# Moving the preparation of the v weights from GpSimd to VectorE in an adaLN attention and FFN block

## The reference

```
mod = (silu(c) @ wmod).reshape(B, 6, 1, 256)           # sa, ca, ga, sb, cb, gb, one set per batch
ga, gb = sign(g) * max(|g|, 0.25)
h = layernorm(x) * (1 + ca) + sa
q, k, v = split(h @ w_qkv + b_qkv)                     # 8 heads of 64
attn = softmax(q^T k / sqrt(64))                       # 64 x 64 per head, summed over the 2048 tokens
out = (v @ attn) @ w_fc + b_fc + h
x = x + ga * (layernorm(out) * gamma + beta)
h = layernorm(x) * (1 + cb) + sb
xr, xk = mu * h + (1 - mu) * h_previous_token
x = x + gb * sigmoid(xr @ W_r) * (relu(xk @ W_k)^2 @ W_v)
```

## Time and profile before

| what | value |
|---|---|
| median of 3 runs | 690.74 us (690.01 to 690.99) |
| profiled execution | 690.6 us, of which the span of the trace is 688.9 us |
| PE busy | 670.7 us, 97% of the span |
| DVE busy | 561.0 us, 81% |
| ACT busy | 393.8 us, 57% |
| POOL busy | 317.5 us, 46% |

### The profile page before, as it was taken

How to read it: one execution, slowest core, us unless ns; L and a number is a source line. 1 busy time by engine, 2 the same in 40 slices (tenths; PEclk the granted TensorE clock), 3 DMA queues, 4 the chain that set the end, 5 groups by cost and what they waited for, 6 DMA issues and landing times.

```text
span 688.9 us, 11754 instructions
## 1 busy us (share of the span) xinstructions
PE 670.7 (97%) x3712; PEld 539.4 (78%) x3712; DVE 561.0 (81%) x1254; ACT 393.8 (57%) x871; POOL 317.5 (46%) x520
## 2 busy tenths in 40 slices
PE   7988999999999999999999999999999999999896
PEld 6777886888778887879868887788878788687674
DVE  5693999789887998889887898979988898658973
ACT  1424575566754675474855667546754747547662
POOL 5272864573254642565335742646325753214320
PEclk9989999999999999999999999999999999999999
DMA  8849345485836666572855849366665528628225
GB/s 316 232 152 222 103 131 123 77 212 97 209 74 142 163 135 147 99 167 92 198 113 79 219 91 213 67 141 158 145 136 99 107 72 173 123 37 179 37 31 91
DMA packets 90984, 93.02 MB, mean 135 GB/s; under 512 B 4224, under 2 KB 89000, under 8 KB 90960
## 3 DMA queue, kind: packets, MB, share of 16 engines
q0 software_dynamic: 33264, 33.03, 32.6%
q1 hardware_dynamic: 55344, 55.97, 25.6%
q10 hardware_dynamic: 2352, 3.73, 1.5%
HBM read 42.84 MB, written 33.10 MB: 110 GB/s over the span
## 4 chain that ended last, share of the span: by engine, by line
PE 86%; DVE 7%; POOL 2%; DMA 2%; issue 1%; ACT 1%; SPq 0%; DVEq 0%; POOLq 0%
PE work L1335 14%; PE work L1318 14%; PE att L1285 13%; PE gram L1267 11%; PE gram L1398 4%; PE att L1370 4%; PE work L1151 4%; PE tr L1260 4%; PE work L1153 4%; PE work L1152 4%; PE tr L1302 4%; PE att L1389 2%; PE gram L1380 1%; PE att L1318 1%; DVE st L907 1%
## 5 line engine op out<-in xcount | busy, mean ns | idle before, releaser
L471 POOL TENSOR_TENSOR rs<-ve,neg_half 128x4 f32<-128x4 f32 x32 | 41.6, 1300 | 161.4 <-DVE ve L917 161.4
L1285 PE MATMUL att<-m_sb,z_t 128*128 128x256 f32 x496 | 112.4, 380 | 1.6 <-issue 0.8
L1335 PE MATMUL work<-mx,w_k_t 128*128 128x512 f32 x236 | 106.2, 592 | 0.0
L1285 PEld LDWEIGHTS att<-m_sb,z_t 128*128 128x128 f32 x496 | 92.4, 190 | 16.9 <-issue 5.7
L1318 PE MATMUL work<-w_r_t,mx 128*128 128x256 f32 x464 | 105.7, 381 | 0.0
L1318 PEld LDWEIGHTS work<-w_r_t,mx 128*128 128x128 f32 x464 | 85.9, 190 | 11.1
L1267 PE MATMUL gram<-z 128*128 128x256 f32 (+1 forms) x512 | 90.7, 331 | 0.0
L1267 PEld LDWEIGHTS gram<-z 128*128 128x128 f32 x512 | 81.1, 194 | 6.9
L934 DVE SCALAR_TENSOR_TENSOR mx<-t_buf,mu_col,h2t 128x512 f32<-128x512 f32 x120 | 84.3, 765 | 1.1
L654 ACT ACTIVATE sq<-att 128x256 f32<-128x256 f32 x124 | 46.1, 383 | 64.1 <-PE att L1285 64.1
L1335 PEld LDWEIGHTS work<-mx,w_k_t 128*128 128x128 f32 x236 | 44.8, 190 | 44.1 <-issue 42.6
(11 more groups left out here) (170 smaller groups left out, 1283.6 us busy)
## 6 DMA issues: line engine op xcount, KB each, us to landing
x_in<-in_L_attn_x_dram SPq DMA_DIRECT2D x32, 512.0 KB, 4.8
x<-rows SPq DMA_DIRECT2D x32, 512.0 KB, 3.4
x<-in_L_attn_x_dram POOLq DMA_DIRECT2D x32, 512.0 KB, 8.9
out_dram<-x SPq DMA_DIRECT2D x31, 512.0 KB, 5.1
out_dram<-y POOLq DMA_DIRECT2D x29, 512.0 KB, 6.2
rows<-row_scratch SPq DMA_DIRECT2D x16, 128.0 KB, 4.1
rows<-row_scratch SPq DMA_DIRECT2D x8, 256.0 KB, 3.8
wqkv_sb<-in_L_attn_w_qkv_dram ACTq DMA_DIRECT2D x1, 1536.0 KB, 9.7
```

Of the source, the lines that this page charges most:

```text
L1285: ins = mm(att_banks(j, alone)[q][:, (t % 2) * D:(t % 2 + 1) * D], z_t[:, j, k, t * P:(t + 1) * P], m_sb[:, k], start=(k == 0), stop=(k == ...
L1335: ins = mm(k_banks(alone)[dh][:], w_k_t[:, ch, rows_dh], mixed(j, alone)[1][:, ch], start=(ch == 0), stop=(ch == KD - 1))
```

## The change

`prep_wv` for batches 1 to 7 goes from GpSimd's list to VectorE's. There it stands behind `low_k(b, 1)` and ahead of `stats_2(b, 3)`, in all of rows 0 to 6. Batch 0 keeps its preparation on GpSimd (`prep_wv()`, `bias_wv()`). In rows 0 to 5 VectorE's steps for batch n + 1 are put in another order among those around the softmax.

```
             def row_steps(b, first, far):              # GpSimd
...
-                    prep_wv(n)
...
-                if first:
-                    prep_wv(n)
...
+            def prep_wv(b):                            # VectorE
+                dve.wait_ge(ca_loaded, 16 * (b + 1))
+                wait_past(dve, m_ready, b)
+                nc.vector.tensor_tensor(wv_aug[:], wv_t[:], rows[:, 3].unsqueeze(1).to_broadcast([P, NP, D]),
+                                        ALU.mult).then_inc(wv_step, 1)
+                dve.wait_ge(wv_step, 2 * b + 1)
+                nc.vector.tensor_tensor(wv_aug[:, :, 0:LAST], wv_aug[:, :, 0:LAST],
+                                        wv_aug[:, :, LAST:D].to_broadcast([P, NP, LAST]), ALU.subtract).then_inc(wv_step, 1)
+                dve.wait_ge(wv_step, 2 * b + 2)
+                nc.vector.tensor_copy(wv_aug[:, :, LAST], vb_col[:, :, b]).then_inc(wv_ready, 1)
...
                 low_k(b, 1)
+                prep_wv(n)
                 stats_2(b, 3)
-                if far:
-                    stats_a(n + 1, 0)
                 gate_o(b, 1)
                 softmax_dif(n)
                 if far:
-                    stats_a(n + 1, 1)
+                    stats_a(n + 1, 0)
                 softmax_norm(n)
                 if far:
+                    stats_a(n + 1, 1)
                     make_z(n + 1, 0)
+                    stats_a(n + 1, 2)
                     make_z(n + 1, 1)
-                    stats_a(n + 1, 2)
                 low_k(b, 2)
                 make_m(n)
```

More of the change, by code:

```diff
@@ L485, in fill_x2, with prep_wv, bias_wv @@
                 nc.gpsimd.dma_start(x2[:, j], x_v[b, j], accum_op=ALU.add).then_inc(x2_filled[j], 16)
[L487 to L495, removed]
+            def prep_wv():
+                pool.wait_ge(w_copied, 2)
+                pool.wait_ge(row8_b_ready, 1)
+                pool.wait_ge(ca_loaded, 16)
                 nc.gpsimd.tensor_tensor(wv_aug[:], wv_t[:], rows[:, 3].unsqueeze(1).to_broadcast([P, NP, D]),
                                         ALU.mult).then_inc(wv_step, 1)
-                pool.wait_ge(wv_step, 2 * b + 1)
+                pool.wait_ge(wv_step, 1)
                 nc.gpsimd.tensor_tensor(wv_aug[:, :, 0:LAST], wv_aug[:, :, 0:LAST],
                                         wv_aug[:, :, LAST:D].to_broadcast([P, NP, LAST]), ALU.subtract).then_inc(wv_step, 1)
-            def bias_wv(b):
-                pool.wait_ge(wv_step, 2 * b + 2)
+            def bias_wv():
+                pool.wait_ge(wv_step, 2)
                 pool.wait_ge(vb_ready, 1)
-                nc.gpsimd.tensor_copy(wv_aug[:, :, LAST], vb_col[:, :, b]).then_inc(wv_ready, 1)
+                nc.gpsimd.tensor_copy(wv_aug[:, :, LAST], vb_col[:, :, 0]).then_inc(wv_ready, 1)
             def add_y(b, j, alone=False):
@@ L571, in _ @@
                 rstd_a(0, j)
-            pool.wait_ge(w_copied, 2)
-            pool.wait_ge(row8_b_ready, 1)
-            centre_wv(0)
+            prep_wv()
             rstd_a(1, 0)
             rstd_a(1, 1)
-            bias_wv(0)
+            bias_wv()
             for j in range(CH):
```

## The result

The kernel after takes 698.62 us (697.52 to 700.22, 4 runs) against 690.75 us (690.01 to 690.99, 4 runs). The ratio is 1.0114, 95% interval 1.0101 to 1.0127: slower by 7.9 us. The direction was forecast. The size was not: 695.7 with a range up to 698.0.

What follows compares the result with a forecast made beforehand. TensorE's list was taken to bound the kernel. In rows 0 to 5 a late `k_lo` costs TensorE 1.12 us less a vanished wait of 0.29: 6 x 0.83 = +5.0 us, forecast 695.7, range 690.2 to 698.0.

Steps and rivals of the forecast that it cites:

- TensorE bounds, and only its waits count: In a row TensorE is busy 80.16 of 80.20 us; VectorE or GpSimd work counts only where TensorE waits.
- The gain on `make_z` at the row's start is worth nothing: VectorE's `make_z` no longer meets GpSimd's v weights and gets back some 2.5 us; effect on time taken as 0.
- The v weights take 2.6 us on VectorE: Behind `low_k(b, 1)`, two instructions of 1.22 us and a small copy, 2.6 us; bounds 1.4 and 5.3.
- `softmax_dif` 1.08 late, the statistics of chunk 0 behind it: On VectorE, `softmax_dif` ends at 358.85, then chunk 0's statistics; the softmax keeps 0.7 us of slack.
- Two `rstd_a` in a row: On GpSimd behind chunk 0's statistics: first 2.31 us to its power, second 1.85; the second value is there at 366.48.
- The second `make_z` beside the DMA issues, 2.13: On VectorE ahead of `low_k(b, 2)`, 2.13 us beside GpSimd's two DMA issues; bounds 1.30 and 3.9.
- The rival at 706: VectorE is blocked for the whole of GpSimd's DMA issues, `k_lo` 2.9 us late, 706 us; chance 0.02.
- What comes back: `m_sb` starts only 0.59 us later, so TensorE's 0.29 wait at `ffn_out(b, 3)` disappears; net 0.83 a row.
- The sum: Rows 0 to 5 at 0.83 us each, +5.0 us; row 6, row 7 and the setup 0.
- The range: 8 in 10: 690.2 to 698.0; the forecast case's own 693.5 to 697.8, with the chain right to 0.35 us a row.
- not slower: Rival: second `make_z` misses the DMA issues and takes 1.30, so `low_k(b, 2)` is on time; 690.7 us, chance 0.21.

Runs made afterwards that it cites:

- e2: Kernel before with only the new order of VectorE's statistics and normalisations, v weights still on GpSimd: 692.77 us, ratio 1.0027.
- e5: Kernel after with the statistics of chunk 2 put ahead of the first `make_z`: 696.84 us, ratio 1.0083.
- e3: Kernel after with GpSimd's `add_y(b, 1)` and `fill_x2(n, 1)` moved behind `rstd_a(n + 1, 2)`: 694.02 us, ratio 1.0052.
- e8: Kernel before with `low_k(b - 1, 3)` put ahead of `prep_qk(n)`, v weights still on GpSimd: 690.22 us, ratio 0.9986.
- e7: e6 with `low_k(b - 1, 3)` put ahead of `prep_qk(n)` at the row's start: 689.29 us, ratio 0.9971 to the kernel before.
- e6: Kernel after with `make_z(n + 1, 1)` moved from in front of `low_k(b, 2)` to the row's end: 691.05 us, ratio 0.9996.
- e1: Kernel after with the old order of statistics and normalisations, v weights still on VectorE behind `low_k(b, 1)`: 695.51 us, ratio 1.0071.
- e4: e1 with the v weights on VectorE moved to the row's start, behind `make_z(n, 2)`: 694.06 us, ratio 1.0045 to the kernel before.

## Why the prediction was right in direction and wrong in size

- **TensorE bounds, and only its waits count**: right. Its busy time is unchanged, and its waits in front of `ffn_out(b, 2)` in rows 0 to 5 (1.24, then 1.39 to 1.41) sum to 8.2 us, against 7.5 more of span.
- **The gain on `make_z` at the row's start is worth nothing**: right. It came (65.1 to 49.9 us in all) and moved no wait: ahead of the next `make_x2` VectorE is idle (2.44 us at 397.55, for `rs_o`).
- **The v weights take 2.6 us on VectorE**: right, 357.35 - 354.68 = 2.67, two at 1.22.
- **`softmax_dif` 1.08 late, the statistics of chunk 0 behind it**: right, 358.90 in place of the 358.85 forecast. The softmax kept its slack, no wait at `wv_attn`.
- **Two `rstd_a` in a row**: the first took 366.17 - 363.87 = 2.30 to its power (2.31 forecast). **The second is the step that failed**: it was priced by one that ran "alone", at 1.85, and took 2.22. In the new order its first operations run beside the first `make_z` (2.22 in e2 as well). e5 puts statistics beside them and gets 1.89. That is 0.37 of the 0.53 by which `k_lo` was later than I said (370.45 against 369.92).
- **The second `make_z` beside the DMA issues, 2.13**: the mechanism was right (e3: 1.40 without them), the size was 2.24 to the next instruction, 0.11 more. With 0.05 from the v weights that makes the 0.53. The rival at 706, by which VectorE stands until the second issue ends, was not borne out: `make_z` ended at 372.62, and the second issue at 371.19 + 1.82 = 373.01. The Trainium skill (SBUF — State Buffer, Who interferes with whom) has the loser of the shared ports fully blocked for the whole instruction of the other; beside these issues the trace does not agree, and `make_z` took 2.21 where it takes 1.38.
- **What comes back**: TensorE's wait is 1.64 in place of 1.12. `m_sb` is 1.10 later (373.86 - 3.49 = 370.37) in place of 0.59. The wait in front of `ffn_out(b, 3)` is gone, as forecast, but for 0.21 in row 1. In row 4 the pair of `k_lo` starts at 392.54 and ends at 393.82, and the load at 393.94 has no idle time before it (lines below the list). Yet only 0.21 of the 0.29 came back. From `attention(4, 1)` at 390.87 to the Gram products at 398.02 it is 7.15, against 6.20 + 0.87 = 7.07 without a wait. The 0.08 is the slower pace of the 24 products, 0.118 us each in place of 0.114, as in e8; e7, whose low part is ready early, has it too. Its cause is open. Net 1.64 - 0.29 + 0.08 = 1.43, against 0.83 forecast.
- **The sum**: six rows at 0.83 made 5.0; row 0 and rows 1 to 5 gave 1.30 + 7.05 = 8.35. Of the 0.60 missed in a row, 0.37 is the second `rstd_a`, 0.11 `make_z`, 0.05 the v weights and 0.08 the pace of `ffn_out(b, 3)`. The setup, row 6 and row 7 gave back 0.85, the part outside the span added 0.5.
- **The range**: 0.35 us a row for the chain's error was too little. A link was taken from a quiet place of the trace and put into a busy one, and six rows multiply each tenth. The bounds of each single cost were wide enough (1.30 to 3.9 for `make_z`), but for `rstd_a` I had given none, though the trace held one at 2.31. With 2.31 for the second as well, the same sum gives 0.46 more a row, 698.5.
- **Two slips in the working**: by its own numbers the late start is 370.20 - 369.10 = 1.10, not 1.12, which is 0.1 us in the sum. And in row 6 two `make_z` are absent beside the three `stats_a`, so VectorE has about 6.6 us less to do there, not 4. The 0 for that row stays right.

VectorE's `k_lo(3, 3)` and TensorE's first load of `ffn_out(3, 3)` in the kernel after:

```profile
392.54 1.28 DVE L934 TENSOR_TENSOR k_lo<-work,k_hi 128x512 fp32r<-128x512 f32 x2
393.94 0.19 PEld L1154 LDWEIGHTS work<-wvf_lo,k_hi 128*128 128x128 f32 x1
```

Of the rivals, "not slower" named the link that matters, but not the size. With 0.8 us out of that link (e3) the loss falls by 0.82 a row and 0.61 is left, since the chain was 0.53 longer than I had summed; with the whole link out (e6) it is gone. The direction was not luck: each wait stands where it was said to. That the forecast lay only 2.9 us off owes something to the setup and the last rows, which gave back 0.85 of what rows 0 to 5 had lost, more than the 0.5 that the part outside the span added.

## What to carry to other kernels

Moving work to an engine with idle time costs by where it stands, not by how much it is: the same 2.7 us of VectorE cost 0.9 to 1.1 us a row ahead of the softmax (e1 against before, after against e2) and about 0.1 behind the row's first `make_z` (e4, which paid 2.6 us once, in row 0) or with one `make_z` moved out of the way (e6). When a chain alternates between VectorE and GpSimd, price each link from an instance that has the same neighbours on the other engine, and where there is none, take the slowest instance in the trace as the bound. An instruction that nobody needs for 20 us (the chunk normalised by 372.62 is transposed from 397.15 on) has no place directly in front of one for which TensorE waits.

## What the runs showed of the hardware that was not expected

- GpSimd's operations on 128 x 4 elements, 0.20 us each, take up to 0.36 beside VectorE's `make_z` (tensor_scalar on 128 x 255; in the kernel after 0.31, 0.24, 0.36 and 0.25 from 367.46 on) and 0.20 beside bn_stats (e5). Beside `attn`'s tensor_tensor (L1022, 364.36) two of them take 0.37 and 0.48. The later ones of the same `rstd_a` run at 0.20 beside a `make_z` (in the kernel before at 361.00, with the `make_z` of the earlier trace rows from 360.63), so it does not hit every operation.
- The other way round, `make_z` takes 1.38 to 1.40 beside `rstd_a`, 2.20 to 2.22 beside the two DMA issues, and in the earlier trace rows 3.89 beside the v weights on GpSimd.
- TensorE's second product follows the end of a late `k_lo` by 0.28 to 0.30 us in row 3 of before, after, e1, e2, e3 and e5 (after: 373.94 to 374.23), the price that the prediction took from one sample.
- The 24 products of one `ffn_out` (128 x 256 each) follow each other at 0.114 us or at 0.118 at the same granted clock of 1.00, by which an `ffn_out` is 0.09 us longer. No run shows what decides.
